# A two-layer graph network: the last bias addition moved, late block visits joined, window positions read sixteen at a time, statistics of y taken in pairs

## The reference, cut to what matters

```python
# layer 0: relational convolution with 4 bases, then ReLU
coeff = w_comp[edge_type]                          # (E, 4)
msg = einsum('ebo,eb->eo', einsum('ei,bio->ebo', x[src], weight), coeff) * edge_weight[:, None]
x1 = layernorm(x + relu(segment_sum(msg, dst) + bias0))
# layer 1: degree-normalised convolution with self loops
ew = concat(edge_weight, ones(N)); deg = segment_sum(ew, dst_with_loops)
agg = segment_sum((1 / deg)[dst] * ew * (x1 @ W)[src], dst_with_loops)
y = layernorm(x1 + agg + bias1)
```

## Time and profile before

| | us |
|---|---|
| median of 3 runs (2087.26 to 2089.07) | 2088.11 |
| the profiled execution, whole | 2089.16 |
| its span in the profile | 2087.3 |
| PE busy | 1565.7 (75%) |
| DVE busy | 1308.7 (63%) |
| ACT busy | 859.7 (41%) |
| POOL busy | 1496.0 (72%) |

### The profile page before, as it was taken

The page is one execution under the profiler, slowest core; times in us unless marked ns, Lnnn a source line. Parts: engine busy times, 40 slices in busy tenths (PEclk is TensorE's granted clock), DMA queues, the critical chain, the costliest instruction groups (busy, mean ns, idle before and its releaser), DMA issues.

```text
span 2087.3 us, 61661 instructions
## 1 busy us (share of the span) xinstructions
PE 1565.7 (75%) x22006; PEld 1250.0 (60%) x22006; DVE 1308.7 (63%) x3680; ACT 859.7 (41%) x2173; POOL 1496.0 (72%) x1590
## 2 busy tenths in 40 slices
PE   3787676767786677777767877787788798888785
PEld 2555455555565455556655666666667676776674
DVE  8885555756656565476555666565765555675556
ACT  4563343544344343344443444343444334453103
POOL 6777777777777777777777777777777777777610
PEclk8888788888878888888888999899999898999896
DMA  5544443434334544455444444544455544555791
GB/s 130 153 146 147 142 140 96 138 125 134 103 120 139 153 145 131 147 148 151 120 139 144 120 143 146 148 144 133 116 164 161 156 123 117 177 165 138 228 346 34
DMA packets 198873, 300.04 MB, mean 144 GB/s; under 512 B 66646, under 2 KB 139531, under 8 KB 192431
## 3 DMA queue, kind: packets, MB, share of 16 engines
q1 hardware_dynamic: 97480, 162.32, 22.1%
q10 hardware_dynamic: 50983, 82.41, 12.8%
q0 software_dynamic: 50112, 51.41, 12.7%
HBM read 187.43 MB, written 108.56 MB: 142 GB/s over the span
## 4 chain that ended last, share of the span: by engine, by line
POOL 51%; issue 22%; PE 17%; DMA 3%; DVE 2%; ACTq 2%; ACT 2%; DVEq 1%; POOLq 0%; SPq 0%
POOL gathered_rows L758 51%; PE coefs_ps L1268 2%; PE coefs_ps L1301 2%; DMA gathered_rows<-in_x,idx 2%; PE node_ps L1178 2%; PE sums_ps L1202 1%; PE sums_ps L1178 1%; PE types_ps L1178 1%; ACTq L588 1%; PE sums_ps L1215 1%; PE dense_ps L1178 1%; ACT room L977 1%; DVE acc_room L2051 1%; DVEq L2039 1%; PE sums_ps L1331 1%
## 5 line engine op out<-in xcount | busy, mean ns | idle before, releaser
L758 POOL DMA_INDIRECT gathered_rows<-in_x,idx x1559 | 1476.0, 947 | 480.9 <-issue 467.3
L1202 PE MATMUL sums_ps<-gathered_rows,chunk_factors 128*32 128x64 f32 x3118 | 139.5, 253 | 363.6 <-issue 189.3
L1787 DVE TENSOR_TENSOR first_room<-first_room,dve_ps 128x1024 bf16<-128x1024 bf16 x585 | 365.2, 679 | 0.0
L1202 PEld LDWEIGHTS sums_ps<-gathered_rows,chunk_factors 128*32 128x32 f32 x3118 | 77.4, 122 | 385.8 <-issue 193.0
L977 ACT COPY room<-dense_ps 128x294 f32 x390 | 168.8, 433 | 325.2 <-PE dense_ps L1178 277.4
L977 ACT COPY room<-node_ps 128x294 f32 x390 | 168.7, 433 | 276.0 <-PE node_ps L1178 156.0
L1781 DVE TENSOR_TENSOR first_room<-dve_ps,first_room 128x1960 bf16<-128x1960 f16 (+2 forms) x260 | 238.8, 939 | 0.0
L1178 PE MATMUL dense_ps<-first_room 128*128 128x245 bf16 x1170 | 217.3, 299 | 27.4 <-DVE first_room L1787 27.3
L1178 PE MATMUL sums_ps<-first_room 128*128 128x245 bf16 (+1 forms) x1170 | 233.0, 311 | 0.0
L1866 DVE TENSOR_TENSOR acc_room<-acc_room,sums_ps 128x88 f32 x196 | 47.8, 244 | 285.1 <-PE sums_ps L1215 277.1
L1809 DVE TENSOR_TENSOR dve_ps<-coefs_ps,edges 128x32 f32<-128x32 f32 x196 | 38.7, 197 | 296.5 <-PE coefs_ps L1163 288.6
(11 more groups left out here) (303 smaller groups left out, 2565.4 us busy)
## 6 DMA issues: line engine op xcount, KB each, us to landing
acc_room<-block_table ACTq DMA_DIRECT2D x147, 374.5 KB
block_table<-room SPq DMA_DIRECT2D x11, 2621.5 KB
type_rows<-in_edge_type SPq DMA_DIRECT2D x260, 96.0 KB
gathered_rows<-in_x,idx POOLq DMA_INDIRECT x1559
block_table<-room SPq DMA_DIRECT2D x9, 2247.0 KB
acc_room<-block_table ACTq DMA_DIRECT2D x56, 321.0 KB
block_table<-room SPq DMA_DIRECT2D x9, 1872.5 KB
block_table<-room SPq DMA_DIRECT2D x10, 1498.0 KB
```

The lines of the kernel that those rows point to most:

```text
L758: pool.indirect_dma_start(gathered_rows[:, s, j, 0:D], None, rows, bass.IndirectOffsetOnAxis(ap=idx[:, s, j:j + 1], axis=0)).then_inc(rows ...
L1202: last = nc.tensor.matmul(parts_ps[lane:lane + LANE, D * k:D * k + D], chunk_factors[:, q, c, :], rows, start=True, stop=True)
L1787: last = nc.vector.tensor_tensor(lo_hot[:, w, q0:q1, :, :], lo_hot[:, 2, q0:q1, :, :], part_of_weights(w), ALU.mult)
```

## The change

All of it concerns the stretch behind the main loop, but for `add_bias(7)`, which is moved into the loop, and the reading of positions, which the loop does too.

- `add_bias(BATCHES - 1)` moves from behind the tail's factors into iteration 64, behind the one-hots of its first step.
- Of the 54 units left over, 25 stay. For the other 29 blocks (27 to 53) the unit of batch 6 is joined with that of batch 7: one load of 8 tiles, one group of 16 matmul instructions, one addition. There are 92 late units: 25, and 67 in REST. `SLOTS` goes from 28 to 27, and a late slot from 535 to 856 words.
- The late units around the last x1 go from (12, 2, then 2 behind `begin_norm`) to 6, 9 and 2 ahead of `take_x1(7)`, 2 ahead of `begin_norm`, 2 behind it. PE does all 25 before it turns the last x1.
- `NEAR = 16`: one read brings the positions of 16 blocks. By the list of units the late stretch has 8 reads (ahead of late units 0, 16, 25, 41, 57, 73, 89 and 90) where it had 32. The sixth last unit of the loop (block 45) had a read ahead of it that goes.
- The over rows are summed behind unit 26 of REST (before 32), the tail rows behind unit 40 (before 32). `transform_near` follows units 28, 33, 38, 43, 49, 57 and 64.
- The statistics of y are finished for batches (0, 1), (2, 3), (4, 5), (6), (7): `begin_norm`, the root and `end_norm` run on 14 columns where they ran on 7, five times where they ran eight.
- `invert_degs` has three instructions in place of four.

```diff
+NEAR = 16
+LATE = (6, 15, 17, 25)
+NORMS_OF_Y = ((0, 1), (2, 3), (4, 5), (6,), (7,))
...
+    late, joined = waiting[:LATE[-1]], [b for b, _, _, _ in waiting[LATE[-1]:]]
...
+        if b in joined:
+            rest.append((b, BATCHES - 2, BATCHES, False))
+        else:
+            rest += [(b, k, k + 1, b >= OPEN[-1] and k == first) for k in range(first, BATCHES)]
...
-SLOTS = 28
-OVER_AT = 32
-TRANSFORM_AFTER = [max(n + 2, OVER_AT + 4 * b + 3) for b, n in enumerate(COMPLETES)]
+SLOTS = 27
+OVER_AT = 26
+TAIL_AT = 40
+TRANSFORM_AFTER = [max(n + 2, OVER_AT + 5 * b + 2) for b, n in enumerate(COMPLETES)]
...
-                nc.vector.tensor_scalar(scratch, degs, 0.0, None, ALU.is_gt)
-                nc.vector.tensor_scalar(to, degs, TINY, None, ALU.max).then_inc(deg_step, 1)
+                nc.vector.tensor_scalar(scratch, degs, TINY, None, ALU.max).then_inc(deg_step, 1)
...
-                nc.vector.tensor_tensor(to, to, scratch, ALU.mult).then_inc(deg_step, 1)
+                nc.vector.scalar_tensor_tensor(to, degs, 0.0, scratch, ALU.is_gt, ALU.mult).then_inc(deg_step, 1)
...
-                        four = range(b - b % 4, min(b - b % 4 + 4, ITERS))
+                        near = range(b - b % NEAR, min(b - b % NEAR + NEAR, ITERS))
...
+                        if s == 0 and i == ITERS - 1:
+                            add_bias(BATCHES - 1)
...
-                add_bias(BATCHES - 1)
                 back(ITERS - 1, 1)
-                for u in range(LATE_AT, LATE_AT + LATE_FIRST):
+                late = [LATE_AT] + [LATE_AT + n for n in LATE]
+                for u in range(late[0], late[1]):
                     add_late(u)
                 back(ITERS - 1, 2)
-                for u in range(LATE_AT + LATE_FIRST, LATE_AT + LATE_SECOND):
+                for u in range(late[1], late[2]):
                     add_late(u)
                 add_window(0, ITERS * U, ITERS * U, 0, U)
+                for u in range(late[2], late[3]):
+                    add_late(u)
                 take_x1(BATCHES - 1, window_ps)
+                for u in range(late[3], late[3] + 2):
+                    add_late(u)
                 begin_norm(0, BATCHES - 1)
-                for u in range(LATE_AT + LATE_SECOND, LATE_AT + LATE_SECOND + 2):
+                for u in range(late[3] + 2, late[3] + 4):
                     add_late(u)
                 end_norm(0, BATCHES - 1)
```

More of the change, by code:

```diff
@@ L140, in plan_visits @@
             steps[i * U + s], waiting = waiting[:n], waiting[n:]
+    late, joined = waiting[:LATE[-1]], [b for b, _, _, _ in waiting[LATE[-1]:]]
+    assert all(unit[1:] == (BATCHES - 2, BATCHES - 1, False) for unit in waiting)
     rest = []
@@ L143, in plan_visits @@
         first = batches_done(b) if b >= OPEN[-1] else BATCHES - 1
-        rest += [(b, k, b >= OPEN[-1] and k == first) for k in range(first, BATCHES)]
-    return steps, waiting, rest
+        if b in joined:
+            rest.append((b, BATCHES - 2, BATCHES, False))
+        else:
+            rest += [(b, k, k + 1, b >= OPEN[-1] and k == first) for k in range(first, BATCHES)]
+    return steps, late, rest
 VISITS, LEFT_OVER, REST = plan_visits()
@@ L337, in partial_of @@
         def partial_of(u):
-            return tile_of(u, BATCH_TILES[UNITS[u][1]])
+            return slots[slot_of[u]][:, UNIT_WORDS[u] - WB:UNIT_WORDS[u]]
         slot_of, used_last, loads_of, loads_until, free_at = [], [], [0] * len(slots), [], {}
-        for u, (b, k, with_partial) in enumerate(UNITS):
+        for u, (b, k, end, with_partial) in enumerate(UNITS):
             if u < BEGUN[-1]:
@@ L548, in nodes_of, with norm_of, stats_at, norm_columns @@
             return slice(FIRST_TILE[b] * P, FIRST_TILE[b + 1] * P)
+        def norm_of(b):
+            return next((n, of) for n, of in enumerate(NORMS_OF_Y) if b in of)
+        def stats_at(layer, b):
+            return norm_of(b)[1].index(b) * BATCH if layer else 0
+        def norm_columns(layer, n):
+            return slice(0, BATCH * len(NORMS_OF_Y[n]) if layer else BATCH)
         def halves_of(b):
@@ L587, in load_unit @@
             queue.wait_ge(blocks_stored[b % 2], 16 * (b // 2 + 1) + 16)
[L588 to L589 removed]
+            queue.dma_start(slots[v][:, 0:(FIRST_TILE[end] - FIRST_TILE[k]) * WB],
+                         block_table[b * P:(b + 1) * P, FIRST_TILE[k] * WB:FIRST_TILE[end] * WB]).then_inc(unit_loaded[v], 16)
             if with_partial:
@@ L1043, in _ @@
                     copy_self(BATCHES - 1, part, bank)
[L1044 to L1048, removed]
+                for n, of in enumerate(NORMS_OF_Y[:-1]):
+                    take_root(1, n)
+                    for b in of:
+                        normalise_all(1, b)
+                        store_y(b)
+                take_root(1, len(NORMS_OF_Y) - 1)
             with act.If(early == 0):
@@ L1435, in _ @@
                 place_parts(ITERS * U, 1, TAIL, U)
+                for u in range(late[2], late[3]):
+                    visit_late(u)
                 pe.wait_ge(window_added, ALL_SUMMED)
                 transform(0, BATCHES - 1, window_ps)
-                for u in range(LATE_AT + LATE_SECOND, TURN_AT):
+                for u in range(late[3], late[4]):
                     visit_late(u)
@@ L1443, in _ @@
                 pe.wait_ge(coefs_weighted, ITERS * U + 1 + U)
-                for u in range(TURN_AT, len(UNITS)):
+                for u in range(REST_AT, len(UNITS)):
                     visit_late(u)
@@ L1993, in begin_norm_of_y, with end_norm_of_y @@
                 take_stats(1, b)
-                begin_norm(1, b)
+                n, of = norm_of(b)
+                if b == of[-1]:
+                    begin_norm(1, n)
+            def end_norm_of_y(b):
+                n, of = norm_of(b)
+                if b == of[-1]:
+                    end_norm(1, n)
             with dve.If(early == 1):
```

127 lines of the change are left out of this document (70 added, 57 removed).

## The result

The kernel with the change takes 2072.14 us (median of 4 runs, 2070.66 to 2075.86) against 2088.28 for the kernel before (4 runs beside it). The ratio is 0.9929, 95% interval [0.9917, 0.9941]. The forecast was 2072 in a range of 2059 to 2085.

What follows compares the result with a forecast made beforehand. POOL's gathers bound the main loop, so gain comes behind it: transform(0) at 2004.5, transform(4) 31 later, take_y(4) at 2039.5, 31.9 more to the span's end at 2071.4, hence 2072 us. Range 2059 to 2085.

Steps and rivals of the forecast that it cites:

- The bias addition: Moved into iteration 64, add_bias(7) takes 0.42 us instead of 6.17 beside POOL's presets; additions replacing it there are not held.
- The bound of 3 us: Kept for the range's upper end, in case window and unit additions beside POOL's presets are held up to 1970.5.
- The read of sixteen: One DVE read of sixteen positions, three words apart, takes 3.5 us; 16 singles then cost 8.2 against 7.4.
- Rival A: A read of sixteen costs only what SP's does, 1.16 us; 13 us go and the end is at 2059; chance 0.20.
- Up to the last x1: First late addition at 1966.7, the tail's window at 1976.6, last x1 done at 1985.9 against 1986.46.
- DVE is through the tail's factors at 1962.8: At the main loop's end, dropping a read ahead of its last units makes DVE 1.0 us earlier.
- To the first transform: After the last x1, over rows land at 2000.4 and transform(0) begins at 2004.5 instead of 2024.84.
- rival C: PE's clock is down from the first read on, singles cost 0.71 us, the end is at 2094; chance 0.08.
- y: Rounds of 5.8 us plus 1.6 for reads, 31 in all: transform(4) at 2035.5, take_y(4) at about 2039.5.
- Rival B: Waits at reads put PE at 1.2 GHz for half of y's rounds, losing 6.3 us: 2079; chance 0.15.
- The last stretch: From take_y(4) to the end of the span takes 31.9 us against 31.1, with 2.5 more for the last read.
- The sum: The span ends at 2071.4; time around it and the profile's offset from the median make it 2072.

Runs made afterwards that it cites:

- e7: The kernel before with only add_bias(7) moved into iteration 64: 2085.32 us, ratio 0.9985 to the kernel before.
- e1: The changed kernel with the blocks' positions copied once into a row side by side, still read by sixteen: 2061.37 us, ratio 0.9882 to the kernel before.
- e4: The changed kernel with the statistics of y finished batch by batch, eight times and not five: 2081.14 us, ratio 0.9977 to the kernel before.
- e3: The changed kernel with no units joined and 28 slots: 2090.47 us, ratio 1.0017 to the kernel before.

## Why the prediction was right, and where it was not

**The bias addition** took 0.47 at 1936.27, forecast 0.42. What stands beside the presets (1963.47 to 1970.10) was not held: the window addition at 1965.36 took 0.23, the units' 0.27. The bound of 3 us for that was not needed. e7 gives the move 3 us alone, with the doubt said there.

The rows now have both halves of the rule cited there (the Trainium skill, SBUF — State Buffer, "Who interferes with whom"): two SBUF operands beside a preset, 6.17; one from PSUM, 0.23 to 0.27. The trace agrees.

**The read of sixteen**: forecast 3.5, measured 3.6, two of the eight 4.0 and 4.1. Rival A is out, yet its 1.16 is near what sixteen numbers cost side by side (1.11, e1).

The floor of about 600 ns (the Trainium skill, DMA: Bandwidth & Descriptors, "Latency and other measured facts") does not hold here: one number takes 0.31 to 0.33 in each of these kernels, and above that the time goes by how many numbers are read and how far apart they lie.

**Up to the last x1**: the first late addition came at 1969.14 (forecast 1966.7), the tail's window at 1977.55 (1976.6), the end of x1 at 1986.78 (1985.9). The step that failed is "DVE is through the tail's factors at 1962.8", 1.0 earlier than before. It was 1965.4, 1.6 later. PE's timeline before, then after: its coefficients, a group behind DVE's one-hots, and the last 90 instructions of the loop.

```profile
1925.78 0.31 PE L1163 MATMUL coefs_ps<-wc_part,type_hot 128*128 128x16 bf16 x6
...
1955.17 5.95 PE L1268 MATMUL coefs_ps<-room,x_nodes 128*64 128x107 f32 x90 [3.32 <-issue]
```

```profile
1927.35 0.31 PE L1186 MATMUL coefs_ps<-wc_part,type_hot 128*128 128x16 bf16 x6
...
1936.41 0.50 PE L1201 MATMUL dense_ps<-first_room 128*128 128x245 bf16 x3 [1.35 <-DVE first_room L1816]
...
1956.63 6.06 PE L1291 MATMUL coefs_ps<-room,x_nodes 128*64 128x107 f32 x90 [2.06 <-issue]
```

The read that leaves gave 1.3 (PE's wait went from 3.32 to 2.06), as forecast. The prediction counted it and left out the one that comes: a read of sixteen stands from 1929.0 to 1932.1 (3.17 idle) ahead of the one-hots that PE's last blocks are built from. PE waits 1.35 for these, and is 3.0 late behind that wait where it was 1.5 late ahead of it. The other 1.6 was there before this read (1927.35 for 1925.78): PE had run at half clock from 1922.6. e1 has the same 1.5 at that place (its group of that kind begins at 1927.31) and no wait for the one-hots, so the long read made one half of the delay and not the other; what brought the half clock on there is open. The prediction said that the main loop matters only where it delays a gather; it also matters in its last two iterations, whose results the tail waits for. From the first late addition to the tail's window it then took 8.4 where 9.9 were forecast, so that the last x1 came out within 0.9: the end was met by two errors of opposite sign.

**To the first transform**: 2007.99, forecast 2004.5. 0.9 is that x1. Behind the second stall (2.86) four single units took 0.71 each in place of 0.37 and the joined one behind them 0.96 in place of 0.73, 1.6 more: rival C's mechanism, but for some 4 us and not for the whole stretch. The first stall, of 2.50, had no such effect. Half clock came ahead of the last x1 too, behind the first read of sixteen and behind the second (0.87 to 0.98 for a single unit in place of 0.53), and the granted clock up to 1987.2 was 0.85, where e1 has 1.00. Of the remaining 1.0 some 0.6 is in the two reads (3.98 and 3.60 of idle DVE for 3.5).

**y**: from transform(0) to transform(4) 26.05, forecast 31. The term was mis-sized: PE's joined unit, 0.735, and its round of 5.45 without a stall were right (5.50 measured from first to second), but I priced two reads of sixteen into these rounds at full length. One of them began with transform(4), at 2033.7, and of the other PE saw 0.92, since four joined units and a transform are 4.7 us of work in hand against 1.5 in single units. Beside that, DVE was the later one at transform(4) only (1.67 at 2034.04). From transform(4) to `take_y(4)` it took 5.7, forecast 4.0, of which the prediction's own rows give only 3.2 (two joined units and a transform): the read of sixteen, 3.57, stood there, and PE ran at half clock. `take_y(4)` came at 2039.76, forecast 2039.5: 3.5 late at the first transform, 5.0 early up to the fifth and 1.7 late behind it cancelled. That the moment was hit is luck in large part.

**Rival B**, the half clock in y: the granted clock was 0.95 there, so it did not hold for half of the rounds, though a read made PE wait 2.5 and 2.9 behind four singles and not 2. It did come once: behind the wait of 1.67 the fifth transform took 2.06 and two joined units 1.48 and 1.36 from start to start in place of 0.73, some 1.7 us in all. e4 has more of it. The prediction's ground for B runs two stretches of the trace of before together. Behind the wait of 1.67 at 2023.17 only four units took 0.71, and PE was at full clock again by 2031.45. The transform of 3.2 that it names, at 2047.8, is the fifth one, and that stretch of half clock began behind waits of 1.49 and 1.86 at 2037.55 and 2039.99.

**The last stretch**: 30.3, forecast 31.9. The last read costs DVE 4.07 of idle time ahead of the last two units, as forecast; PE waits 2.83 for it at the last transform, where e1 waits 0.47. The rest came out 1.6 shorter, which was not taken apart.

**The sum**: span 2070.1, forecast 2071.4. The parts as measured by taking each out (joining 18, pairing 9, y earlier 5 to 7, reads of sixteen about -6) or putting it in (bias 3) don't add to 16; each changes PE's waits and clock in the stretches of the others.

## What to carry to other kernels

Price a blocking read by what its engine's neighbours have in hand while it lasts: the same 3.6 us cost PE 2.9 behind four single units and 0.9 behind joined ones (2.7 there in e4, where DVE came to it later). A part of a change that looks like the saving can be its loss: fewer and longer reads lost 6 us, and laying the numbers side by side won 10. Compare marks that the edit can touch, stretch by stretch, before a difference between spans is put down to it: 4.4 of e3's delay lay ahead of the stretch that its edit works on. Where a loop's end feeds a tail, check what is added in the last iterations too, however idle the engine is in the loop's mean.

## What the runs showed that was not expected

- Of reads into DVE's registers, one of sixteen numbers takes 3.6 us where they lie three words apart and 1.11 side by side; of four, 0.96 and 0.35; of one, 0.31 to 0.33.
- The length of a stall alone did not tell whether half clock followed: with the change, one of PE of 2.50 left the granted clock up and one of 2.86 nine us later was followed by four units at half speed, then by full speed again without a pause; one of 1.67 was followed by half speed too, and in e3 one of 2.83 (at 2025.94) was not.
- The same kernel takes 2088 us on some chips and 3163 on two others, with the gathers at 947 to 948 ns on both and PE standing for "issue".
